# A mixed scan, attention and feed-forward network: one decay in a lent PSUM bank, the attention norm by tokens, and a new order of the loop

## The reference

```python
# layer 0: x = x + mamba(group_norm(x, 32 groups))
xm, z = split(u @ in_proj_w.T)                    # 192 inner channels each
xm = silu(causal_conv4(xm) + conv_b)
dt, Bm, Cm = split(xm @ x_proj_w.T)               # 6, 16, 16
delta = softplus(dt @ dt_proj_w.T + dt_proj_b)
h = exp(delta * A) * h + delta * Bm * xm          # scan over the 4096 positions, 192 x 16 states
y = (sum over states of Cm * h + xm * D) * silu(z)
out = layernorm(y @ out_proj_w.T) * gamma + beta
# layer 1: t = t + attn(ln(t)) ; t = t + ffn(ln(t))
attn = (q k^T) v / 4 without softmax, 6 heads     # so k^T v is a 96 x 96 matrix for each image
ffn = q_acc(W2 q_mul(relu(q_acc(W1 q_mul(.)))))   # products in fp8 (5, 2), sums rounded to fp16
```

## Time and profile before

| | us |
|---|---|
| median of 3 runs | 2523.43 (2519.72 to 2525.91) |
| the profiled execution | 2516.53 |
| its span, first to last instruction | 2514.7 |

### The profile page before, as it was taken

One profiled execution on the slowest core, in us unless ns is written; L12 is line 12 of the kernel. 1 busy time (PEld: TensorE's weight loads), 2 busy tenths in 40 slices (PEclk: granted clock), 3 DMA queues, 4 the chain that ended last, 5 costly groups with the idle time before them and its releaser, 6 DMA issues.

```text
span 2514.7 us, 34499 instructions
## 1 busy us (share of the span) xinstructions
PE 2097.2 (83%) x10022; PEld 776.5 (31%) x10022; DVE 2456.7 (98%) x2391; ACT 2316.0 (92%) x3960; POOL 2419.2 (96%) x719
## 2 busy tenths in 40 slices
PE   6687777888888888888888888888888888888878
PEld 3222222323333323323333323323333333333323
DVE  7999999999999999999999999999999999999986
ACT  5777777999999999999999999999999999999977
POOL 4999999999999999999999999999999999999991
PEclk8888999999999999999999999999999999999979
DMA  6555555656656566666566566566566566566542
GB/s 240 191 184 174 191 185 182 203 199 206 208 201 208 203 203 202 208 206 214 197 208 209 197 211 207 196 213 209 191 216 208 188 216 203 181 215 206 175 137 74
DMA packets 171386, 494.51 MB, mean 197 GB/s; under 512 B 23072, under 2 KB 44704, under 8 KB 154240
## 3 DMA queue, kind: packets, MB, share of 16 engines
q1 hardware_dynamic: 171200, 492.30, 58.3%
HBM read 400.33 MB, written 91.88 MB: 196 GB/s over the span
## 4 chain that ended last, share of the span: by engine, by line
DVE 67%; issue 13%; POOL 13%; ACT 4%; PE 3%; DMA 1%; DVEq 0%; POOLq 0%; ACTq 0%; SPq 0%
DVE R L1271 50%; DVE D L1255 10%; POOL R L669 9%; POOL D L648 2%; DVE q L1351 1%; ACT DA L834 1%; DVE G L1296 1%; DVE dl L1281 1%; DVE yv L1292 1%; POOL D L657 1%; PE G L1562 1%; DVE th L1304 1%; PE Y L1643 0%; POOL du L641 0%; DVE G L1330 0%
## 5 line engine op out<-in xcount | busy, mean ns | idle before, releaser
L1271 DVE TENSOR_TENSOR_SCAN R<-DA,R,D 128x512 f32<-128x512 f32 x1344 | 1630.0, 1263 | 1.5 <-ACT DA L834 1.5
L669 POOL TENSOR_TENSOR R<-R,Cs 128x2048 f32<-128x2048 f32 x383 | 1453.4, 3817 | 0.0
L834 ACT ACTIVATE DA<-ds,kept_w 128x512 f32<-128x512 f32 x1536 | 1054.6, 688 | 144.2 <-DVE R L1271 130.6
L648 POOL TENSOR_TENSOR D<-us,Bs 128x2048 f32<-128x2048 f32 x193 | 736.8, 3818 | 9.5 <-DMA us<-lo_d 9.5
L1255 DVE TENSOR_TENSOR D<-us,PB 128x2048 f32<-128x2048 f32 x191 | 358.9, 1879 | 7.0 <-DMA us<-lo_d 7.0
L1639 PE MATMUL Y<-R,kept_w 128*32 128x512 f32 x2048 | 273.8, 628 | 26.3 <-POOL R L669 26.3
L1596 PE MATMUL G<-un,wcv 96*128 96x512 f32 x512 | 251.7, 614 | 29.4 <-ACT h L901 29.4
L1271 DVE TENSOR_TENSOR_SCAN R<-DA,D 128x512 f32<-128x512 f32 x192 | 221.7, 1205 | 2.0 <-ACT DA L834 2.0
L1599 PE MATMUL G<-un,wcv 96*64 96x256 f32 x1024 | 138.1, 391 | 59.3 <-ACT xq L882 57.7
L1562 PE MATMUL G<-st,kept_w 128*64 128x256 f32 (+1 forms) x384 | 110.0, 489 | 63.2 <-ACT st L796 63.2
L1562 PE MATMUL G<-sq,kept_w 96*96 96x512 f32 (+1 forms) x256 | 137.2, 618 | 28.5 <-DVE dl L1281 27.2
(11 more groups left out here) (237 smaller groups left out, 3259.0 us busy)
## 6 DMA issues: line engine op xcount, KB each, us to landing
Bs<-bc_d SPq DMA_DIRECT2D x128, 512.0 KB, 5.3
us<-lo_d SPq DMA_DIRECT2D x64, 1024.0 KB, 6.5
ds<-lo_d SPq DMA_DIRECT2D x64, 1024.0 KB, 8.5
Cs<-bc_d SPq DMA_DIRECT2D x128, 512.0 KB, 4.8
us<-hi_d SPq DMA_DIRECT2D x64, 512.0 KB, 6.9
ds<-hi_d SPq DMA_DIRECT2D x64, 512.0 KB, 5.4
lo_d<-dl SPq DMA_DIRECT2D x64, 256.0 KB, 2.0
lo_d<-du SPq DMA_DIRECT2D x64, 256.0 KB, 2.0
```

Of the source, the lines that this page charges most:

```text
L648: nc.gpsimd.tensor_tensor(shaped(D[:, s % NDBU, :, :], s), low(us, s) if s in LOWS else high(us), of_states(Bs, s), ALU.mult).then_inc(don ...
L669: nc.gpsimd.tensor_tensor(shaped(R[:, s, :, 0:T], s), shaped(R[:, s, :, 1:S], s), of_states(Cs, s), ALU.mult).then_inc(hc_done.sem, 1)
L834: nc.scalar.activation(DA[j % NDA][:, :], ds[:, i, :], ACT.Exp, scale=A[:, j:j + 1]).then_inc(exp_done.sem, 1)
L1271: nc.vector.tensor_tensor_scan(R[:, s, q, 1:S], DA[j % NDA][:, :], D[:, s % NDBU, q, :], before, ALU.mult, ALU.add).then_inc(scanned.sem, 1)
```

## The change

**A bank is lent.** decay(g,1,0) goes into G0 instead of DA0, and its scan reads it there. TensorE's list says when G0 is free: it waits for G0's last reader and raises a semaphore (`lend`). decay(g,1,2), the next user of DA0, then waits only for the scan four before it.

**The attention norm by tokens.** TensorE now makes the centred x1 already transposed (`centre_by_token`, four products of 96 columns) and the variance as one column for each 128 tokens (`variance_by_token`); ScalarE takes Ln and Exp on 128 x 4 and multiplies the four pieces by their column (`token_ln`, `token_std`, `token_scale`) into tT. TensorE transposes tT back (`from_tokens`), and ScalarE copies that to th (`th_copy`). VectorE's token_norm, one 96x512 variance product, Ln and Exp and the token copy go. The 96x512 centre and square stay.

**eps as a row.** sq and fsq get a 97th row of ones and avg a row of 1e-5, so Ln needs no bias.

**TensorE copies B for quad 1.** put_b(g,1) is a product of a selection matrix with st, no longer a copy on ScalarE.

**Split 296** instead of 240: VectorE takes 296 columns of quad 3, GpSimd 216.

**Order.** GpSimd does product(g,1) before delta_u(g+1), and product(g,2) before inputs(g,5). Every other engine's iteration is reordered; z_proj comes before the convolution in part, and TensorE gets short `spin` products in iterations where the feed-forward part is missing (0 < g < 10 to 12). SyncE's order is kept; keep_th waits for th_copy.

```diff
-FRONT = (3, 1, 4, 2)
-SPLIT = {3: 240}
+FRONT = (4, 2, 1, 3)
+SPLIT = {3: 296}
+BORROWS = 4
...
             def keep_th(k):
-                    sp_eng.wait_ge(post_dve.sem, post_dve.at(k, 2))
+                    sp_eng.wait_ge(th_done.sem, th_done.at(k))
...
                     product(g, 0)
                     inputs(g, 4)
+                    product(g, 1)
                 if there(g + 1):
                     delta_u(g + 1)
                 if there(g):
-                    product(g, 1)
+                    product(g, 2)
                     inputs(g, 5)
-                    product(g, 2)
                     product(g, 3)
                     product(g, 4)
...
-            def decay(k, s, q):
+            def decay(k, s, q, borrowed=None):
...
+                if borrowed is not None:
+                    act.wait_ge(lent.sem, lent.at(k))
+                elif j - NDA == BORROWS:
+                    act.wait_ge(scanned.sem, scanned.at(k, j + 1 - 2 * NDA))
+                else:
+                    act.wait_ge(scanned.sem, scanned.at(k, j + 1 - NDA))
+                to = DA[j % NDA] if borrowed is None else borrowed
...
+            def token_ln(k, src):
+                act.wait_ge(tok_mm.sem, tok_mm.at(k, 2))
+                act.wait_ge(post_act.sem, post_act.at(k - 1, 5))
+                nc.scalar.activation(rsT[:, :], src[:, 4 * C:4 * C + T // 128], ACT.Ln).then_inc(post_ln.sem, 1)
...
+            def token_scale(k, src):
+                act.wait_ge(post_act.sem, post_act.at(k, 4))
+                act.wait_ge(post_mm.sem, post_mm.at(k - 1))
+                act.wait_ge(th_mm.sem, th_mm.at(k - 1))
+                for a in range(T // 128):
+                    last = nc.scalar.activation(tT[:, a, 0:C], src[:, a * C:(a + 1) * C], ACT.Identity, scale=rsT[:, a:a + 1])
+                last.then_inc(post_act.sem, 1)
+
+            def th_copy(k, src):
+                act.wait_ge(th_mm.sem, th_mm.at(k))
+                if there(k - 1):
+                    act.wait_ge(th_out, kept(k - 1))
+                nc.scalar.copy(th[0:C, :], src[0:C, :]).then_inc(th_done.sem, 1)
...
             def ending():
                 k, m = LAST, LEFT[0] - 1
-                inv_std(k - 1, 1)
+                token_std(k - 1)
+                token_scale(k - 1, G0)
                 for h in range(2):
                     last_square(0, h, DA[h])
-                token_copy(k - 1, G0)
+                th_copy(k - 1, G0)
...
-            def token_norm(k, o):
-                dve.wait_ge(post_act.sem, post_act.at(k, 4))
-                dve.wait_ge(post_mm.sem, post_mm.at(k - 1, 5))
-                if there(k - 1):
-                    dve.wait_ge(th_out, kept(k - 1))
-                nc.vector.tensor_tensor(th[0:C, :], o[0:C, :], rs[:, :], ALU.mult).then_inc(post_dve.sem, 1)
...
+            def put_b(k, s):
+                if k == 0 and s == 1:
+                    return
+                pe.wait_ge(st_done.sem, st_done.at(k))
+                pe.wait_ge(dbu_d.sem, dbu_d.at(k, BY_DVE[s] - steps_to(k, s)))
+                one(PB[:, :], state_row[32:64, (1,).index(s), :], st[32:64, :]).then_inc(b_put.sem, 1)
...
+            def centre_by_token(k, o):
+                pe.wait_ge(x1_done.sem, x1_done.at(k))
                 for a in range(T // 128):
+                    last = one(o[:, a * C:(a + 1) * C], x1[:, a * 128:(a + 1) * 128], cen)
+                last.then_inc(tok_mm.sem, 1)
...
+            def variance_by_token(k, o):
+                pe.wait_ge(post_act.sem, post_act.at(k, 3))
+                for a in range(T // 128):
+                    last = one(o[:, 4 * C + a:4 * C + a + 1], sq[:, a * 128:(a + 1) * 128], avg[:, 0:1])
+                last.then_inc(tok_mm.sem, 1)
...
+            def from_tokens(k, o):
+                pe.wait_ge(post_act.sem, post_act.at(k, 5))
+                for a in range(T // 128):
+                    last = nc.tensor.transpose(o[0:C, a * 128:(a + 1) * 128], tT[:, a, 0:C], eye)
+                last.then_inc(th_mm.sem, 1)
...
+            def lend(k):
+                pe.sem_inc(lent.sem, 1)
```

More of the change, by code:

```diff
@@ L217, in build @@
         x1 = xq[0:C, :]
-        sq = sb("sq", [C, T])
+        sq = sb("sq", [C + 1, T])
         rs = sb("rs", [C, T])
@@ L952, in iteration @@
                 if there(g):
-                    decay(g, 1, 2)
+                    decay(g, 1, 3)
+                if inside(g - 11):
+                    output(g - 11, G0)
+                if there(g):
+                    decay(g, 2, 0)
+                if there(g + 2):
+                    norm(g + 2)
+                if there(g):
+                    decay(g, 2, 1)
                 if there(g + 1):
@@ L1030, in iteration @@
                 if there(g):
+                    decay(g, 5, 0)
+                if there(g - 1):
+                    square(g - 1, 1, G0)
+                if there(g):
                     decay(g, 5, 1)
-                if there(g - 1):
-                    inv_ln(g - 1, 1, G2)
+                if place(g + 3) == 0 and later(g + 3):
+                    group_scale(g + 3, PB, 2)
                 if inside(g - 10):
-                    hidden_bias(g - 10, 1)
-                    hidden(g - 10, 2, G2)
+                    hidden_bias(g - 10, 0)
                 if there(g):
@@ L1360, in iteration @@
                     scan(g, 0, 0)
+                    scan(g, 0, 1)
                 if there(g - 1):
                     gate(g - 1, 0)
-                if there(g - 2):
-                    token_norm(g - 2, G0)
+                if there(g):
+                    scan(g, 0, 2)
                 if place(g + 3) == 0 and later(g + 3):
@@ L1382, in iteration @@
                 if there(g):
+                    scan(g, 1, 1)
+                    scan(g, 1, 2)
                     scan(g, 1, 3)
                     scan(g, 2, 0)
+                if place(g - 10) == 0 and early(g - 10):
+                    fold(g - 10, 4, G0)
+                if there(g):
                     scan(g, 2, 1)
-                if there(g + 1):
-                    delta(g + 1, *((G3, G0) if g < 0 else (G0, G3)))
-                if there(g):
                     scan(g, 2, 2)
@@ L1418, in iteration @@
                 if there(g):
+                    scan(g, 5, 0)
+                    scan(g, 5, 1)
                     scan(g, 5, 2)
+                if there(g + 1):
+                    inputs(g + 1, 0)
+                if there(g):
                     scan(g, 5, 3)
@@ L1818, in iteration @@
                         freed(dl_done, 0)
+                    (freed(th_done, g - 2) or freed(silued, g + 1))
                     x_proj(g + 1, G3)
-                if inside(g - 11):
-                    ((place(g - 10) == 0 and freed(fold_ev, g - 10, 4)) or freed(silued, g + 1))
-                    down(g - 11, G1)
+                if place(g - 10) == 0 and early(g - 10):
+                    (freed(f_y16, g - 11) or freed(scanned, g, 5))
+                    fold(g - 10, 4, G0)
+                if there(g - 1):
+                    (freed(f_out, g - 12) or freed(silued, g + 1, 3))
+                    out_proj(g - 1, G1)
@@ L1843, in iteration @@
-                if there(g - 1):
+                    ((place(g - 10) == 0 and freed(fold_ev, g - 10, 4)) or freed(f_y16, g - 11)
+                     or freed(scanned, g, 5))
+                    variance(g - 1, G0)
+                if there(g):
+                    sum_states(g, 0)
+                if 0 < g < 10:
+                    (freed(post_ln, g - 1, 1) or (place(g - 10) == 0 and freed(fold_ev, g - 10, 4))
+                     or freed(f_y16, g - 11) or freed(scanned, g, 5))
+                    spin(2, G0, *weights)
@@ L1844, in iteration @@
+                if inside(g - 10):
+                    (freed(post_ln, g - 1, 1) or (place(g - 10) == 0 and freed(fold_ev, g - 10, 4))
+                     or freed(f_y16, g - 11) or freed(scanned, g, 5))
+                    centre_tokens(g - 10, G0)
+                if 0 < g < 10:
+                    spin(2, G0, *weights)
+                if inside(g - 10):
+                    centre_x1(g - 10, G0)
+                if place(g - 9) == 0 and early(g - 9):
                     freed(dl_done, g + 1)
-                    variance(g - 1, 0, G3)
+                    fold(g - 9, 1, G2)
@@ new lines, in iteration @@
+                if 0 < g < 10:
+                    (freed(f_ln, g - 10) or freed(dl_done, g + 1))
+                    spin(1, G3, *weights)
+                if inside(g - 10):
+                    (freed(f_ln, g - 10) or freed(dl_done, g + 1))
+                    up(g - 10, 1, G3)
+                if there(g):
+                    sum_states(g, 2)
+                if there(g - 1):
+                    (freed(f_h16, g - 10, 1) or freed(f_q8, g - 10) or freed(post_ln, g - 1, 1)
+                     or (place(g - 10) == 0 and freed(fold_ev, g - 10, 4)) or freed(f_y16, g - 11)
+                     or freed(scanned, g, 5))
```

(1 more changed line is left out.)

409 lines of the change are left out of this document (204 added, 205 removed).

## The result

The changed kernel takes 2552.1 us (median of 4 runs, 2548.8 to 2559.4). The kernel before, run beside it, takes 2524.5 (4 runs, 2519.7 to 2525.9). The ratio is **1.012, 95% interval [1.010, 1.015]**: slower by 28 us, where the forecast was 2508 with a range to 2530. The direction is that of the third rival, and its 2535 was still too low. Two executions further down, one of the 29 of the kernel before that ran beside e5 to e8 (3620.7 us at a granted clock of 0.693, the same program) and one of e8's twelve (2836.8 us, 0.746), ran in a slower state and are left out of the ratios.

The account below looks back on a forecast made before the run. VectorE and GpSimd, both full, were taken as the bound. A gain of 14.0 us from 52 iterations at 0.27, plus 3.9 in early iterations, minus 2.7 at the end, made 15.2 us: 2508 us, range 2498 to 2530.

Parts of the forecast that it names:

- third rival: ds lands 1 us past its due time, ScalarE and scan(0,1) stall; period 37.8, 2535 us, slower; chance 0.13.
- What bounds the kernel: Long stretch: VectorE and GpSimd both full; after the change VectorE's limit 37.21 us an iteration, just above GpSimd's 37.14.
- The prices: Per-iteration instruction costs: GpSimd -0.40 us, VectorE -0.36, ScalarE -0.2 with ends of -1.6 and +1.0.
- the second estimate in the prediction: Trainium skill formula for ScalarE's 96-column products from PSUM: 223 ns each, four times 0.9 us.
- ScalarE becomes the bound: Rival: ScalarE's small products cost 0.4 us each and it idles 0.3 for ds; period 37.5, 2520 us; chance 0.22.
- The lent bank: Around silu, ScalarE writes decay(1,2) at once, so its 0.46 us wait for scans can go; put_b causes no stall.
- It can close up: GpSimd's first product starts 1.05 us after scans allow, so du could start at t + 22.1 instead of t + 23.1.
- three slacks of about zero: Waits for B, ds and inputs 5 after the later du; with fold iterations 0.05 to 0.15 us per iteration, taken 0.09.
- a coin toss: ScalarE's wait for ds: lands at t + 34.4 to 36.5, due by t + 35.2.
- The clock: TensorE's granted clock of 0.53 between 2396 and 2404 us, at the end: from -4 to +4 us, taken as 0.
- The end: Last iteration: th now made later by ScalarE delays the load TensorE awaits, costing +2.7 us.
- The start: Two one-row memsets and a wider weight load beside the input load: between 0 and +1.5 us, taken as 0.

Follow-up runs that it names:

- e5: Changed kernel with SyncE loading B first and ds ahead of us, and hidden_round before decay(g+1,0,0) on ScalarE: 2526.4 us, ratio 1.002.
- e8: e2 plus 14 idle TensorE matmuls in the first iteration and, at the end, x1 and th loads ahead of keep_th: 2509.8 us, ratio 0.997.
- e7: Kernel before with only the split of quad 3 moved from 240 to 296: 2536.1 us, ratio 1.006.
- e2: Changed kernel with one swap on ScalarE, hidden_round before decay(g+1,0,0): 2517.6 us, ratio 1.000.

## Why the prediction was wrong

- **What bounds the kernel: right.** VectorE first, GpSimd just under. e7 measured 37.81 us for 0.24 us more on VectorE, and the changed kernel's short iterations are 37.10 to 37.3 against limits of 37.14 and 37.21.
- **The prices: right,** each within 0.1 us. A piece of tT takes 335 ns alone and 255 in a row of four, where the second estimate in the prediction had 223. *ScalarE becomes the bound* is refuted: busy 1828.1 of 1936 us, which by 38.26 us an iteration is 36.1 where before it was 36.7.
- **The lent bank: right in its own terms.** No wait of the size of the earlier trace rows's 0.46 is a pattern of the new kernel. But it tied TensorE's put_b to ScalarE's token copies. I had tT done by t + 2.0 and counted no stall. That holds only if ScalarE begins the iteration on time; the 32.6 us show it doesn't.
- **"It can close up" by 1 us: the first wrong step.** I read that GpSimd's first product starts 1.05 us after its scans allow. But `rest` stands ahead of it and needs scan(g,0,3). A row of VectorE's timeline of the kernel before, which I had passed over:

```profile
1359.47 4.80 DVE L1271 TENSOR_TENSOR_SCAN R<-DA,R,D 128x512 f32<-128x512 f32 x4
```

  The first of these four is that scan. At 1.27 long it ends at 1360.74, and `rest` starts at 1360.82. There was no play. In the new kernel `rest` mostly starts right behind the scan, and du lies 13.2 us behind `rest` (1342.37 to 1355.58) where it was 9.6: later by 3.6, against 3.4 forecast and 2.4 hoped for.
- **The cost of three slacks of about zero: the step that decided.** The text named each wait, its due time and "a coin toss", then took 0.09 us for all three together. Against the limit of 37.21 the steady mean of the profiled execution is 1.05 higher; by the medians (44 us over the forecast, 52 iterations, and the 0.09 taken) it is about 0.9. Of the 1.05, 0.41 is in iterations like the 37 in which the clock did not fall; the other 0.64 comes with the 16 in which it did. A wait that goes either way half the time, on an engine with four others in a ring with it, has as its price the length of the wait and what it sets off (here falls of the clock too), not a tenth of it. Even with e2's order the steady mean stayed 0.1 above 37.3.
- **The third rival: right in mechanism, its price too small and its chance (0.13) far too small.** ds landed 9.1 us after issue in the median and 10.0 in the long iteration; ScalarE waited for it 50 times, 1.4 us in the mean. The two loads of the earlier trace rows did not hold the spread: in the same trace of before, the load issued at 812.1 took 10.1 us. Its price came only to 37.8, since it had neither tT's hold on TensorE nor the longer matmuls behind a wait. The estimate from the Trainium skill ("DMA: Bandwidth & Descriptors", "Anatomy of one DMA") gave 8 us from B's issue to the last landing; in the long iteration it was 12.0 (1398.66 to 1410.7), and the measurement decides.
- **The clock** was the term put at nothing: it stood in the prediction only for the end. It belonged to every wait of TensorE: the row of 0.53 showed that such stretches exist. In the steady part, where none was forecast, there are 16.
- **The end: right in its term** (TensorE's wait for tn 3.47 instead of 0.94, +2.5 for +2.7 forecast), but the last iteration also had `rest` wait 3.1 us. **The start** was taken as 0 to 1.5, and the early iterations as a gain of 3.9; up to the first steady du the trace is 4.5 us longer. With e2's order the one low-clock stretch there was worth 8 us. Most of the miss lies in the steady part (36.4 of the 42.9 us between the traces).

## What to carry to other kernels

When engines have no slack, a wait whose due time falls inside the spread of a DMA's landing is not a matter of a tenth of a microsecond: price it by what stands behind it on its own queue and by who waits for that, around the ring. Look for the one instruction that can go ahead of the waiting one; here 1.47 us moved by one place was worth 1.2% of the kernel, and moving two more past the same wait gained nothing. If TensorE stands in the ring, look at the granted clock iteration by iteration: a mean of 0.98 hid 16 falls. Before saying that an engine can close up, check every instruction between it and its next free place.

## What the runs showed of the hardware

- TensorE's clock fell to 0.50 in 16 of 53 iterations of an engine that was busy 91% of the stretch, each time at or shortly behind the end of a wait of 0.8 to 2.1 us. Not every such wait is followed by a fall: of its 27 waits for tT in the steady part, nine are.
- Idle matmuls are not free even where TensorE has 8% of air: 1.42 us of them in each iteration, ahead of a copy that others wait for, made the shortest iteration 0.59 us longer and the whole 11 us longer, though they kept the clock at 1.00. An idle fp32 matmul of 256 columns took 0.45 to 0.47 us (6.3 us for 14, 1.42 us for three), as two records.
- After a wait of 4.20 us TensorE's clock stayed at 0.50 from 70 to 80 us while it was busy 5.00 of every 5.00 us; with 14 fillers in that wait it was 1.00 over the same stretch.
- One reordering on GpSimd moved the same program from 2552 to 3570 us, with the granted clock at 0.73: a ring of queues in order can settle at a period 1.5 times its work (54.9 us in the mean against 37.2), and stay there.
- A fixed shape of 96 columns with a column of scales costs 335 ns on ScalarE, four in a row 1.02 us.
